# A graph layer on one core: roots on VectorE, GpSimd adds part of the residual

## The reference, cut to what matters

```python
h = relu(layernorm(x))                        # x: 100000 x 160, no learned scale
s, v = h[:, :64], h[:, 64:].reshape(N, 32, 3)
skip_s, skip_v = s @ W_skip0, einsum('nmi,mk->nki', v, W_skip1)
s, v = s @ W_nl0, einsum('nmi,mk->nki', v, W_nl1)
w = relu(edge_feature @ W_fc1) @ W_fc2        # 25000 edges, 224 weights each
tp = products(w, s[dst], v[dst], edge_attr / norm(edge_attr))     # 480 per edge
agg = segment_sum(tp, src, num_segments=N) / 32
out_s = agg[:, :96] @ W_out_s + skip_s
out_v = einsum('nmi,mk->nki', agg[:, 96:].reshape(N, 128, 3), W_out_v) + skip_v
fs, gate = silu(out_s[:, :64]), sigmoid(out_s[:, 64:96])
out = x + concat([fs, gate[:, :, None] * out_v])
```

## Time and profile before

| | us |
|---|---|
| median of 3 runs | 1369.47 (1368.71 to 1371.86) |
| profiled execution | 1372.43 |
| its span, first to last instruction | 1370.6 |

### The profile page before, as it was taken

How to read it: one execution, slowest core, us unless ns; L and a number is a source line. 1 busy time by engine, 2 the same in 40 slices (tenths; PEclk the granted TensorE clock), 3 DMA queues, 4 the chain that set the end, 5 groups by cost and what they waited for, 6 DMA issues and landing times.

```text
span 1370.6 us, 33958 instructions
## 1 busy us (share of the span) xinstructions
PE 1213.3 (89%) x8857; PEld 995.2 (73%) x8857; DVE 1214.9 (89%) x4487; ACT 1004.9 (73%) x2379; POOL 983.2 (72%) x1135
## 2 busy tenths in 40 slices
PE   4999968999999999986888888888888888888886
PEld 2455537888888888875777777777777777777775
DVE  7999967888889888766999999999999999999996
ACT  3999966788888888855777777767677777767774
POOL 4333347788778888517888888888888888888883
PEclk9999988999999999998999999999999999999998
DMA  3000002344443444325787878778787778878774
GB/s 108 1 0 0 0 20 63 106 112 111 108 112 109 113 109 110 98 69 135 221 238 224 230 229 228 227 226 242 213 240 223 234 225 229 232 224 239 225 230 131
DMA packets 90920, 212.27 MB, mean 155 GB/s; under 512 B 15030, under 2 KB 56281, under 8 KB 90878
## 3 DMA queue, kind: packets, MB, share of 16 engines
q1 hardware_dynamic: 62462, 155.23, 35.9%
q0 software_dynamic: 28416, 56.56, 18.3%
HBM read 127.73 MB, written 84.00 MB: 154 GB/s over the span
## 4 chain that ended last, share of the span: by engine, by line
POOL 42%; PE 29%; issue 17%; DVE 7%; ACT 2%; DMA 1%; DVEq 1%; POOLq 0%; ACTq 0%; SPq 0%
POOL mg L565 32%; POOL n_rstd L571 8%; PE bank L1161 5%; PE bank L1098 4%; PE bank L1214 3%; PE bank L1190 3%; PE bank L1178 3%; PE bank L1145 2%; PE bank L1174 2%; PE bank L1176 2%; DVE rank_junk L717 2%; PE bank L1198 2%; ACT hn L962 2%; DVE bin_hot L681 1%; PE bank L1218 1%
## 5 line engine op out<-in xcount | busy, mean ns | idle before, releaser
L565 POOL DMA_INDIRECT mg<-messages,slot_m x392 | 453.6, 1157 | 121.1 <-issue 110.0
L1035 ACT ACTIVATE nn<-xb,n_bias,n_rstd 128x160 f32<-128x160 f32 x588 | 299.5, 650 | 111.3 <-DVE n_bias L662 109.8
L1240 PE MATMUL bank<-wsk_a,nt_a 128*128 128x160 f32 x1568 | 298.4, 313 | 55.0 <-DVE ob L845 53.2
L1240 PEld LDWEIGHTS bank<-wsk_a,nt_a 128*128 128x128 f32 x1568 | 226.7, 192 | 75.9 <-issue 52.0
L498 POOL DMA_INDIRECT xg<-x,dst_g x200 | 208.2, 1041 | 62.3 <-issue 57.1
L1042 ACT ACTIVATE nt_a<-bank 128x512 f32<-128x512 f32 x196 | 117.0, 597 | 105.8 <-PE bank L1233 105.8
L1254 PE MATMUL bank<-mg,hot 64*128 64x192 f32 x1568 | 181.2, 350 | 11.7 <-DVE hot L832 11.7
L644 DVE BATCH_NORM_STATS2 n_stat<-xb 128x6 f32<-128x160 f32 x784 | 186.7, 312 | 3.7 <-DMA xb<-x 3.4
L1232 PE MATMUL bank<-ident,nn 128*128 128x128 f32 x784 | 147.5, 311 | 35.2 <-ACT nn L1035 30.0
L1232 PEld LDWEIGHTS bank<-ident,nn 128*128 128x128 f32 x784 | 110.2, 210 | 91.6 <-issue 54.0
L571 POOL TENSOR_TENSOR n_rstd<-n_sum,neg_half 128x8 f32<-128x8 f32 x98 | 163.7, 1670 | 12.7 <-DVE n_sum L658 10.6
(11 more groups left out here) (172 smaller groups left out, 2724.4 us busy)
## 6 DMA issues: line engine op xcount, KB each, us to landing
xb<-x SPq DMA_DIRECT2D x97, 640.0 KB, 5.9
out_dram<-ob SPq DMA_DIRECT2D x97, 640.0 KB, 3.5
messages<-msg SPq DMA_DIRECT2D x50, 390.6 KB
mg<-messages,slot_m POOLq DMA_INDIRECT x392
ef<-edge_feat_t SPq DMA_DIRECT2D x50, 125.0 KB, 5.9
xg<-x,dst_g POOLq DMA_INDIRECT x200
xb<-x SPq DMA_DIRECT2D x1, 420.0 KB
out_dram<-ob SPq DMA_DIRECT2D x1, 420.0 KB
```

Source lines behind the costliest of these rows:

```text
L565: pool.indirect_dma_start(mg[:, u, k, :], None, messages[:, :], bass.IndirectOffsetOnAxis(ap=slot_m[:, u, k:k + 1], axis=0)).then_inc(n.g[ ...
L1035: last = act.activation(nn[:, u % 2, h, :, g % 4], xb[:, u, g, :], ACT.Relu, bias=n_bias[:, u, g:g + 1], scale=n_rstd[:, u, g:g + 1])
L1240: pe.matmul(z[:, t, 0:F], nt_a[:, h, t * P:(t + 1) * P], wsk_a[:], start=(t % 2 == 0), stop=False, skip_group_check=True)
```

## The change

1. **Roots.** POOL's `pow` in the node stage goes. The statistics of four macros (32 columns) are collected by bn_stats in three of four rounds (10, 11 and 11 instructions, none in the fourth), and in the fourth round DVE runs 18 small instructions on 128x32: six for the variance, a shift and a multiply for a first guess by bits, three Newton steps of three, and the bias. `n.ln` is raised once for four macros.
2. **Buffers.** `xb` has 8 buffers instead of 4, and SP loads seven macros ahead instead of three (seven at the start, too). Loops are unrolled by 8.
3. **Gates.** ACT computes tanh(z/2) of the 32 gate columns into a smaller `sg` (128x128) and SiLU of 64 columns straight into `ob` (128x256). DVE adds 1 to `sg` in place and multiplies the vector part; the scalar part L844 goes. Half of each weight is folded into the weights (two more small scalings). ACT, no longer DVE, waits for the earlier store of `ob`.
4. **Residual.** DVE adds rows 0 to 5 (128x960), POOL rows 6 and 7 (128x320), ahead of its fetch of the round. SP's store waits for both.
5. **One-hots of the nodes.** Two tensor_tensor of 128x256 with broadcast inputs instead of four tensor_scalar of 128x128.
6. **Binning.** The `slot_v` of every fifth tile is made by one POOL tensor_scalar (125x128) instead of two activations.
7. **End of binning.** The last matmuls close the banks themselves, the edge vectors and weights come ahead of the wait for the table, PE waits only until DVE and ACT have read the four banks (`b_free`), and the rest of the table is made after DVE's first edge round. The opening work of the nodes is spread over the last three edge rounds.

```diff
-U = 4
-xb = sb("xb", [P, U, G, F])
-n_stat = sb("n_stat", [P, U, G, 6])
-n_sum = sb("n_sum", [P, U, 5, G])
-n_rstd = sb("n_rstd", [P, U, G])
-n_bias = sb("n_bias", [P, U, G])
+U, XU = 4, 8
+LV = 16
+RG = 6
+AHEAD = (10, 21)
+SEED = 1597463007.0
+xb = sb("xb", [P, XU, G, F])
+n_stat = sb("n_stat", [P, 2, U * G, 6])
+n_sum = sb("n_sum", [P, 2, 5, U * G])
+n_seed = sb("n_seed", [P, 2, U * G], I32)
+n_step = sb("n_step", [P, 2, 2, U * G])
...
-sg = sb("sg", [P, 2, 4, SG])
+sg = sb("sg", [P, 2, 4, V])
...
-                wait(pool, b_slot, t - BR + 1)
+                wait(pool, b_slot, (BR - BR // BATCH) * (q - 1) + k - k // BATCH)
...
+                r = k % BLOCK
+                wait(pool, b_tab, t - BLOCK + 1)
+                pool.wait_ge(b_dec, n + 1)
+                pool.sem_inc(s_held, 1)
+                pool.tensor_scalar(slot_v[:, r, :], iota_slot[0:ET, :], slot[:, k:k + 1], row_no[:, r:r + 1],
+                                   ALU.is_equal, ALU.mult).then_inc(b_last, 1)
...
+            def residual(i, u):
+                pool.wait_ge(n.mul, 2 * i + 2)
+                o = ob[:, u % U, RG:G, :]
+                pool.tensor_tensor(o, o, xb[:, u, RG:G, :], ALU.add).then_inc(n.res_p, 1)
...
-            def ln_n(i, u):
-                pool.wait_ge(n.var, i + 1)
-                pool.tensor_tensor(n_rstd[:, u, :], n_sum[:, u, 4, :], neg_half[:, :], ALU.pow).then_inc(n.pw, 1)
...
-                    ln_n(i + 2, (u + 2) % U)
+                if macro_exists(i - 1):
+                    residual(i - 1, (u + 7) % XU)
+                if macro_exists(i + 2) and not every:
+                    fetch(i + 2, (u + 2) % XU)
             macros(pool, round_n)
+            residual(NM - 1, (NM - 1) % XU)
...
+        dve.wait_ge(b_tab, NT)
+        dve.tensor_scalar(whole[:], p_cnt[(NT - 1) % 2], 1.0 / W_EVEN, None, ALU.mult).then_inc(b_free, 1)
         dve.wait_ge(b_rows_sb, 1)
         for r in range(2):
-            last = dve.scalar_tensor_tensor(out=empty[:, r, :], in0=p_tab[r], scalar=0.0, in1=empty[:, r, :],
-                                            op0=ALU.is_gt, op1=ALU.mult)
-        link(last)
-        dve.tensor_scalar(most[:, 2:3], most[:, 1:2], SHARE, None, ALU.mult)
-        for r in range(2):
-            last = dve.scalar_tensor_tensor(out=tab_row[:, r, :], in0=empty[:, r, :], scalar=2.0 * BLOCK * ET,
-                                            in1=tab_row[:, r, :], op0=ALU.mult, op1=ALU.add)
-        link(last)
-        dve.tensor_tensor(most[:, 3:4], most[:, 0:1], most[:, 2:3], ALU.max)
-        link(dve.tensor_tensor(empty[:, 0, :], tab_row[:, 0, :], tab_row[:, 1, :], ALU.add))
-        dve.tensor_copy(most_i[:], most[:, 3:4])
-        dve.tensor_scalar(slots_i[:], empty[:, 0, :], float(ET * NT), None, ALU.min).then_inc(b_fin, 1)
+            dve.scalar_tensor_tensor(out=empty[:, r, :], in0=p_tab[r], scalar=0.0, in1=empty[:, r, :],
+                                     op0=ALU.is_gt, op1=ALU.mult).then_inc(b_free, 1)
+        def table():
+            dve.wait_ge(b_free, 3)
...
+            def halve(i, u):
+                b, base = u // U, level(i, u)
+                dve.wait_ge(n.root, base + 4)
+                dve.tensor_scalar(n_seed[:, b, :], n_sum[:, b, 4, :].bitcast(I32), 1, None,
+                                  ALU.logical_shift_right).then_inc(n.root, 1)
+            def seed(i, u):
+                b, base = u // U, level(i, u)
+                wait(dve, n.norm, 2 * (i - U))
+                dve.wait_ge(n.root, base + 5)
+                dve.tensor_scalar(n_rstd[:, b, :].bitcast(I32), n_seed[:, b, :], -1.0, SEED, ALU.mult,
+                                  ALU.add).then_inc(n.root, 2)
+            def root_a(i, u, k):
+                b, base = u // U, level(i, u) + 3 * k
+                y = n_rstd[:, b, :]
+                dve.wait_ge(n.root, base + 7)
+                dve.tensor_tensor(n_step[:, b, 0, :], y, y, ALU.mult).then_inc(n.root, 1)
+            def root_b(i, u, k):
+                b, base = u // U, level(i, u) + 3 * k
+                dve.wait_ge(n.root, base + 8)
+                dve.scalar_tensor_tensor(out=n_step[:, b, 1, :], in0=n_step[:, b, 0, :], scalar=-0.5,
+                                         in1=n_sum[:, b, 4, :], op0=ALU.mult, op1=ALU.mult).then_inc(n.root, 1)
+            def root_c(i, u, k):
+                b, base = u // U, level(i, u) + 3 * k
+                y = n_rstd[:, b, :]
+                dve.wait_ge(n.root, base + 9)
+                dve.scalar_tensor_tensor(out=y, in0=n_step[:, b, 1, :], scalar=1.5, in1=y,
+                                         op0=ALU.add, op1=ALU.mult).then_inc(n.root, 1)
+            def shift_n(i, u):
+                b, base = u // U, level(i, u)
+                dve.wait_ge(n.root, base + 16)
+                shift(n_bias[:, b, :], n_sum[:, b, :, :], n_rstd[:, b, :]).then_inc(n.ln, U)
...
+                bins = slice(2 * half, 2 * half + 2)
+                made = dve.tensor_tensor(hot[:, u % 2, bins, :], iota_local[:].unsqueeze(1).to_broadcast((P, 2, P)),
+                                         mg[:, m, bins, LOCAL:LOCAL + 1].to_broadcast((P, 2, P)), ALU.is_equal)
...
-                dve.tensor_tensor(o[:, :, 0:S], z[:, :, 0:S], sg[:, h, :, 0:S], ALU.mult)
+                o = ob[:, u % U, 4 * h:4 * h + 4, :]
+                dve.tensor_scalar(sg[:, h, :, :], sg[:, h, :, :], 1.0, None, ALU.add).then_inc(n.one, 1)
+                dve.wait_ge(n.fs, 2 * i + h + 1)
...
-                dve.tensor_tensor(ob[:, u, :, :], ob[:, u, :, :], xb[:, u, :, :], ALU.add).then_inc(n.res, 1)
+                o = ob[:, u % U, 0:RG, :]
+                dve.tensor_tensor(o, o, xb[:, u, 0:RG, :], ALU.add).then_inc(n.res, 1)
...
+                before, after = (u + 7) % XU, (u + 1) % XU
+                j, w = i + 2, (u + 2) % XU
+                extract = u % U == 2 and macro_exists(j)
                 if macro_exists(i - 1):
+                    gate(i - 1, before, 1)
+                if extract:
+                    spread(j, w)
                 if macro_exists(i + 1):
+                    norm_last(i + 1, after)
+                if extract:
+                    squares(j, w)
                 if macro_exists(i - 1):
+                    residual(i - 1, before)
+                if extract:
+                    variance(j, w)
                 if macro_exists(i + 1) and not every:
+                    hot_n(i + 1, after, 0)
+                    if extract:
+                        halve(j, w)
+                    hot_n(i + 1, after, 1)
+                elif extract:
+                    halve(j, w)
+                if extract:
+                    seed(j, w)
+                    root_a(j, w, 0)
+                    root_b(j, w, 0)
+                    root_c(j, w, 0)
+                    root_a(j, w, 1)
+                if u % U == 3 and macro_exists(i + 5):
+                    stats_n(i + 5, (u + 5) % XU, 0, AHEAD[0])
+                if u % U == 0 and macro_exists(i + 4):
+                    stats_n(i + 4, (u + 4) % XU, AHEAD[0], AHEAD[1])
+                if u % U == 1 and macro_exists(i + 3):
+                    stats_n(i + 3, (u + 3) % XU, AHEAD[1], U * G)
                 if every:
                     places(i)
                 gate(i, u, 0)
+                if extract:
+                    root_b(j, w, 1)
+                    root_c(j, w, 1)
+                    root_a(j, w, 2)
+                    root_b(j, w, 2)
+                    root_c(j, w, 2)
+                    shift_n(j, w)
...
+            if k % BATCH < BATCH - 1:
+                done, s = (BR - BR // BATCH) * q + k - k // BATCH, (k - k // BATCH) % 2
+                act.wait_ge(b_dec, BR // BATCH * q + k // BATCH + 1)
...
-                act.activation(sg[:, h, :, :], q_z[h][:, :, 0:SG], ACT.Sigmoid).then_inc(n.sg, 1)
+                act.activation(sg[:, h, :, :], q_z[h][:, :, S:SG], ACT.Tanh, scale=0.5).then_inc(n.sg, 1)
+                act.activation(ob[:, u % U, 4 * h:4 * h + 4, 0:S], q_z[h][:, :, 0:S], ACT.Silu).then_inc(n.fs, 1)
...
-        for o in (*p_cnt, *p_tab):
-            last = pe.matmul(o, zeros_h[0:ET, 0:o.shape[0]], zeros_h[0:ET, :], start=False, stop=True,
-                             skip_group_check=True)
-        last.then_inc(b_end, 1)
-        pe.wait_ge(b_fin, 1)
+        pe.wait_ge(b_free, 3)
```

More of the change, by code:

```diff
@@ L738, in _ @@
-                dve.reduce_max(most[:, 1:2], rest[:], AX_X)
+                dve.wait_ge(s_sqrt, 1)
+                link(dve.reciprocal(vec_r[:], vec_r[:]))
+                link(dve.tensor_tensor(vec_n[:, 0, :], vec_r[:], vec_d2[:], ALU.mult))
+                link(dve.tensor_tensor(vec_n[:, 1, :], vec_n[:, 0, :], vec_r[:], ALU.mult))
+                link(dve.tensor_scalar(vec_n[:, 0, :], vec_n[:, 1, :], -0.5, 1.5, ALU.mult, ALU.add))
+                link(dve.tensor_tensor(vec_r[:], vec_r[:], vec_n[:, 0, :], ALU.mult))
```

321 lines of the change are left out of this document (179 added, 142 removed).

## The result

The changed kernel takes 1376.86 us (median of 20 runs, 1368.26 to 1382.38), the kernel before beside it 1371.88 (20 runs). The ratio is 1.0038, with a 95% interval of 1.0024 to 1.0051: 0.4% slower, where 1308.5 us was forecast. The profiled execution has a span of 1375.3 us.

A forecast was written before the change was run, and what follows sets the result against it. POOL was taken to bound the node stage at 7.49 us a macro, DVE close behind. A period of 6.95 gives -51 us and binning -10, so 1370.6 becomes 1309.6 of span, forecast as a 1308.5 us median, range 1284 to 1344.

The forecast's parts named there:

- part 5: End of binning: PE starts the edges at 196.2, 7.4 us earlier; 10 us gained in all (2 to 12).
- part 3: Node stage: new loop from gate through POOL's residual, gathers, landing and one-hots to gate; (8.8 + 5.0) / 2 = 6.9 us a period.
- The sign that was named for the loop: Node stage: DVE waiting for `mg` before its one-hots would show that the loop through the gathers binds.
- The landing, 2.1 us: Node stage: time from the end of a fetch to DVE's use of it, 2.1 of the loop's 8.8 us.
- pulls level with the other two: Node stage: the gather loop at 6.9 us equals DVE's 6.9 and POOL's 6.85; the period was taken as 6.95.
- The collision on VectorE, 0.1 us: Node stage: DVE's residual held by POOL's, 0.2 us at worst, 0.1 taken, raising DVE's period to 6.9 us.
- VectorE's own work: Node stage: DVE's sum per macro after the change, without collisions, 6.82 us, between 6.65 and 7.0.
- the port takes more than it gives: Node stage rival: residuals and gathers collide, 0.5 us more on POOL and the loop; period 7.3, 1341 us, chance 0.21.
- The slower case: Node stage rival: collisions cost POOL over 2.3 us a macro beyond 5.85; 8.6 us a period, 1465 us, chance 0.03.
- tables' rival: Node stage rival: tanh and SiLU need four table loads per macro, 5.1 us more on ACT; about 1675 us, chance 0.03.

The follow-up runs named there:

- h2: The changed kernel with GpSimd's gathers issued ahead of its residual, nothing left out; 1328.60 us, 0.9696 of the kernel before.
- m2: The changed kernel storing only the first of each eight output rows, the others left out; 1343.88 us, 0.9807 of the kernel before.
- h5: The changed kernel with GpSimd still waiting for the gate but adding nothing, residual rows 6 and 7 left out; 1352.33 us, 0.9855 of the kernel before.
- m1: The changed kernel with GpSimd's residual still first, but gathers fetched three macros ahead instead of two; 1328.19 us, 0.9685 of the kernel before.
- a0: The changed kernel unaltered, run again as the mark for the kernels beside it; 1377.36 us, 1.0050 of the kernel before.
- g4: The changed kernel with GpSimd's addition and its wait for the gate both removed, residual rows 6 and 7 left out; 1273.74 us, 0.9296 of the kernel before.
- h3: The changed kernel with gathers first and GpSimd's residual also waiting for the next macro's one-hots; 1341.56 us, 0.9771 of the kernel before.
- e1: The changed kernel with all eight residual rows on VectorE, on a chip where the kernel before takes 1457 us; 1462.29 us, ratio 1.0012.

## Why the prediction was wrong

Right:
- *The end of binning* (part 5). PE at 196.90, forecast 196.2; 11.3 us gained up to the first one-hots, forecast 10.
- *The change without its residual on GpSimd.* With the residual back on VectorE (g1) the kernel gains 66 us, some 11 of them ahead of the nodes, and DVE then sets a period of 6.96. What the roots are worth by themselves was not tried. That g1 comes so near to the forecast (1305.3 against 1308.5 us) is luck: the forecast was for a kernel with the residual shared.
- *Tables.* Two loads of 1.28 us, none in the loop. The page "ScalarE: Activation LUTs" of the Trainium skill, section "Table sets: the hidden batching unit", does not list SiLU; here tanh and SiLU alternate in one loop without a load.
- *The shape of the loop* (part 3): gate, residual, gathers, landing, one-hots, gate, over two periods. Its VectorE part was given as 5.0 and is 4.96. The sign that was named for the loop, DVE's wait for `mg` ahead of the one-hots, is there.

Wrong, by its own steps:
- **The landing, 2.1 us, is the term that failed.** It was taken from the first fetch of the stage, when no store and no load of `xb` was under way. In the steady state it is 3.76. With 1.14 for the residual and its wakes in place of 0.73, and 5.55 for the gathers in place of 6.0, the loop is (10.45 + 4.96) / 2 = 7.71 us and not 6.9. With a landing of 2.1 and all else as measured it would be (8.79 + 4.96) / 2 = 6.88, an estimate, and less than the 7.18 that h2 has without the loop. m2 shows a part of the landing to be the load of the stores, and h5, h2 and m1 that the wait in the loop is what counts. The page "DMA: Bandwidth & Descriptors" of the Trainium skill, section "Latency and other measured facts", says that access to HBM takes longer at high load, and that a lighter load lowers the fixed part of a transfer; 3.80 against 3.02 us agrees in sign.
- **A loop that "pulls level with the other two" was taken to cost 0.05 us**, the step from 6.9 to 6.95. Cutting it (h2, m1) gives 7.18 us, 0.53 less than 7.71. Before, the gathers had all the time between: POOL's fetch was bound to no gate. The change made it so, and no cover was asked for.
- *The collision on VectorE, 0.1 us.* Only VectorE's own residual was looked at, and that kept its length (1146 ns). What comes first behind the gate is `norm_last`: 637 ns each in place of 453 (a0, g1), so 2 x 0.18 = 0.37 us, and the sum of L888, 0.89 in place of 0.21 in every fourth round, 0.17. Together 0.54; h2 against g4 gives 7.18 - 6.60 = 0.58. The page "SBUF — State Buffer", section "Who interferes with whom", of the Trainium skill has both: `tensor_scalar` in a 2-port mode and a GpSimd instruction block each other fully, and whichever issues first keeps the ports; and an instruction with two SBUF inputs contends with a GpSimd instruction that reads SBUF. The trace agrees: in the turn shown the two instructions of `norm_last` end at 1013.33, right after GpSimd's addition at 1013.15. bn_stats does not meet the addition in the changed kernel; in h3, where it does, it took 309 ns beside it and 311 elsewhere, in line with the page's rule for one input. The prediction used the section for POOL and not for DVE.
- *VectorE's own work*, 6.82 without collisions, is at most 6.60, the period of g4, in which TensorE is as good as full. Which of its terms was too large was not taken apart.
- *The rivals.* The second, "the port takes more than it gives", had the right kind of mechanism, but asked 0.5 us of it and ended at 1341; the loop that starts from the landing stood in none. The slower case asked for 2.3 us on POOL's own sum, where by its own figures (7.6 less 5.85) 1.75 would do, and POOL's sum never bound. The price of the tables' rival, about 1675 us, is 1661 by the sum that the others use (94 x 3.21, less 10); neither slip changes the forecast or the range.

From g4 over h2 to a0 the period goes 6.60, 7.18, 7.71 us: 0.58 with the addition behind the gathers, 0.53 more with the loop. The two steps add up to the whole by construction; what speaks for the first being collisions is that the lengths give 0.54. In the other order, g4 over h5 to a0, the wait comes to 0.87 and the addition to 0.24, so the two overlap, and neither has one price. What part of the 0.53 is TensorE's lower clock was not tried by itself.

## What to carry to other kernels

Work that is put ahead of a prefetch on an in-order queue brings its wait with it: price that wait, and not only the work. Here the wait cost 79 us without the work (h5 against g4) and 49 on top of it (a0 against h2); the work cost 25 and 55 us. Give the prefetch one more stage, or put it first. A transfer's landing is read from the steady state, under the loads that it will meet, never from the first one of a stage. Where an engine helps another, look at what the helped one does at that very moment: the two rows of residual saved VectorE 0.33 us and took 0.54 from it.

## What was not expected of the hardware

- An addition of 128x320 on GpSimd takes 907 ns in a0, beside `norm_last`, and 868 ns elsewhere (h3); VectorE adds the same 320 columns in 0.33 us, as 1481 against 1148 ns shows.
- GpSimd's gathers take 1078 ns on average in g4, 1147 in a0 and 1174 in g1, which has no addition on GpSimd either but the long residual on VectorE. It is one of the four that is long: in a0 the 76 that start beside VectorE's two-input residual take 1.72 us on average (1.85 in the turn shown), the others 0.96. The section "Who interferes with whom" of the page "SBUF — State Buffer" of the Trainium skill says that tensor_tensor does not hold up descriptor generation; here the long gather starts beside it, in the turn shown above as in the earlier trace rows. By the measurement the rule doesn't hold for these gathers.
- The same program differs by 6% between chips (1371 and 1457 us before). Ratios between kernels shift with it: the edit of e1 and g1 reads 1.0012 on one and 0.9528 on the other.
